# Dense mixtures of a small network: two bank pairs for the sums, high halves on ACT, router from halves, first weights split early

## The reference

```python
# mixture 0 (1 and 3 alike with gelu; 3 has a ninth, shared expert)
logits = jnp.einsum('btc,ce->bte', x, Wg)
probs = jax.nn.softmax(logits, axis=-1)
top_vals, top_idx = jax.lax.top_k(probs, TOP_K)                # TOP_K = 2, 8 experts
gates = (jax.nn.one_hot(top_idx, E, dtype=probs.dtype) * top_vals[..., None]).sum(-2)
h = jax.nn.relu(jnp.einsum('btc,ech->bteh', x, W1) + b1)       # 192 -> 768
y = jnp.einsum('bteh,ehc->btec', h, W2) + b2                   # 768 -> 192
out = jnp.einsum('bte,btec->btc', gates, y)
# mixture 4: (silu(x Wg) * (x Wu)) Wd, 384 hidden channels; mixture 2: capacity 64 per expert
```

## Time and profile before

| | us |
|---|---|
| median of 3 runs | 475.11 |
| lowest and highest run | 474.66, 476.07 |
| profiled execution | 478.6 |
| its span | 476.8 |
| PE matmuls busy in it | 447.4 |
| DVE busy | 337.3 |
| ACT busy | 232.0 |
| POOL busy | 138.4 |

### The profile page before, as it was taken

How to read it: one execution, slowest core, us unless ns; L and a number is a source line. 1 busy time by engine, 2 the same in 40 slices (tenths; PEclk the granted TensorE clock), 3 DMA queues, 4 the chain that set the end, 5 groups by cost and what they waited for, 6 DMA issues and landing times.

```text
span 476.8 us, 9352 instructions
## 1 busy us (share of the span) xinstructions
PE 447.4 (94%) x3260; PEld 385.6 (81%) x3260; DVE 337.3 (71%) x764; ACT 232.0 (49%) x591; POOL 138.4 (29%) x175
## 2 busy tenths in 40 slices
PE   8998999999999899999999897999899999989997
PEld 6776899997676889998677575746699999979997
DVE  3676989995475989996475377421498999887674
ACT  1485455641285665641195058132266565455452
POOL 6011466561011465561001101020055656300000
PEclk9999999999999999999999799999999999999999
DMA  5760155610670155720599403306026566325550
GB/s 156 263 131 2 67 202 154 218 57 1 227 211 1 68 174 174 210 72 0 162 239 246 114 1 92 109 1 231 1 74 211 163 198 197 126 91 182 185 200 20
DMA packets 19364, 62.38 MB, mean 131 GB/s; under 512 B 4041, under 2 KB 6914, under 8 KB 19330
## 3 DMA queue, kind: packets, MB, share of 16 engines
q1 hardware_dynamic: 19330, 61.93, 42.0%
HBM read 59.82 MB, written 2.10 MB: 130 GB/s over the span
## 4 chain that ended last, share of the span: by engine, by line
PE 60%; issue 16%; DVE 7%; ACT 6%; DMA 5%; POOL 3%; SPq 1%; POOLq 0%; DVEq 0%
PE bank L997 23%; PE bank L1005 10%; PE bank L1017 7%; ACT probs L546 5%; PE bank L1019 3%; PE bank L799 2%; PE bank L824 2%; DMA rel<-rel_scratch 2%; PE bank L731 2%; POOL rstd L407 2%; DMA w<-in_M_w_dram 2%; PE bank L692 1%; PE bank L780 1%; PE bank L838 1%; PE bank L974 1%
## 5 line engine op out<-in xcount | busy, mean ns | idle before, releaser
L997 PE MATMUL bank<-xT_hi,w_hi 128*128 128x256 f32 x408 | 109.2, 289 | 1.6 <-issue 1.6
L1282 DVE TENSOR_TENSOR w_lo<-w,w_hi 128x512 fp32r<-128x512 f32 x102 | 96.9, 988 | 2.1
L631 ACT ACTIVATE hid<-bank,b 128x256 f32<-128x256 f32 x150 | 62.8, 471 | 68.7 <-PE bank L997 68.5
L997 PE MATMUL bank<-xT_hi,w_lo 128*128 128x256 f32 x408 | 82.0, 282 | 0.0
L997 PEld LDWEIGHTS bank<-xT_hi,w_hi 128*128 128x128 f32 x408 | 77.9, 191 | 3.9 <-issue 3.8
L460 POOL TENSOR_TENSOR w_hl<-w,consts 128x384 fp32r<-128x384 f32 x50 | 52.5, 1050 | 73.6 <-PE bank L1019 69.9
L997 PEld LDWEIGHTS bank<-xT_hi,w_lo 128*128 128x128 f32 x408 | 63.4, 191 | 0.0
L462 POOL TENSOR_TENSOR w_hl<-w,w_hl 128x384 fp32r<-128x384 f32 x50 | 59.0, 1179 | 3.9
L1005 PE MATMUL bank<-w,hid 128*128 128x192 f32 x308 | 56.4, 327 | 2.5 <-issue 2.5
L583 ACT ACTIVATE w_hi<-w 128x512 fp32r<-128x512 f32 x102 | 58.3, 627 | 0.0
L997 PE MATMUL bank<-xT_lo,w_hi 128*128 128x256 f32 x204 | 57.7, 283 | 0.0
(11 more groups left out here) (169 smaller groups left out, 661.3 us busy)
## 6 DMA issues: line engine op xcount, KB each, us to landing
w<-in_M_w_dram SPq DMA_DIRECT2D x34, 768.0 KB, 5.6
w<-in_M_w_dram SPq DMA_DIRECT2D x33, 576.0 KB, 4.0
w<-in_M_w_dram SPq DMA_DIRECT2D x9, 288.0 KB, 2.9
wqkv<-in_A_wqkv_dram SPq DMA_DIRECT2D x4, 432.0 KB, 7.1
rel_scratch<-relall SPq DMA_DIRECT2D x4, 372.0 KB, 2.3
wproj<-in_A_wproj_dram SPq DMA_DIRECT2D x4, 288.0 KB, 8.3
wqkv<-in_M_w_dram SPq DMA_DIRECT2D x2, 576.0 KB, 23.6
rel<-rel_scratch SPq DMA_DIRECT2D x10, 96.0 KB
```

Of the source, the lines that this page charges most:

```text
L631: ins = act.activation(hid[:, 2 * b + c, :], bank[B_H[b]][:, c * T:(c + 1) * T], FUNC[cfg["act"]], bias=b1[:, kb, bass.ds(at, 1)])
L997: ins = pe.matmul(bank[B_H[b]][:, c2 * T:(c2 + 1) * T], w, xs, start=(q == 0), stop=(q == 4))
L1282: dve.tensor_tensor(w1_cols(w1_lo, b), w1_cols(w1[s], b), w1_cols(w1_hi, b).bitcast(F32), ALU.subtract)\
```

## The change

Five edits, all in the dense mixtures:

1. The sums of even and odd experts go to two bank pairs, (3, 4) and (7, 6). PE waits for the addition of the unit before the last one. In units 0 and 1 DVE makes both units' halves before it adds either sum. The product with the biases b2 moves from bank 6 to 5.
2. `hid_hi` is made by ACT, right after the pair's activation, and no longer by DVE.
3. The router takes the input from `xT_hi` and `xT_lo`, in six matmuls, and the copies to `xT` are gone in dense mixtures.
4. The low half of a mixture's first weights is started ahead of its norm: two parts at the end of attention 0 and 1, all three inside mixture 2 for mixture 3, one at the end of mixture 3 for mixture 4. ACT's high halves stand where they stood.
5. `xn` is written once. The second transpose reads its channels 64 to 191, and the low half of the last 64 channels goes to the lower partitions.

```diff
+EARLY = {0: 2, 1: 2, 3: HB, 4: 1}
...
-        B_H, B_Y, B_R, B_B2 = (0, 1, 2), (3, 4), 5, 6
+        B_H, B_Y, B_R, B_B2 = (0, 1, 2), ((3, 4), (7, 6)), 5, 5
...
@@ ACT: attn, end
+                if n < 2:
+                    for b in range(HB):
+                        split(n, 0, 0, b)
@@ ACT: expert
                             ins.then_inc(h_ready, 1)
+                        if cfg["split2"] and b >= HB - SB:
+                            sb2 = 2 * (b - (HB - SB))
+                            act.wait_ge(h_ready, 3 * (2 * j + g) + b + 1)
+                            act.activation(hid_hi[:, sb2:sb2 + 2, :], hid[:, 2 * b:2 * b + 2, :], ACT.Copy).then_inc(hid_hi_ready, 1)
...
@@ PE: router
+                            terms = ((xT_hi[:, 0, tok].bitcast(F32), 0), (xT_lo[:, tok].bitcast(F32), 0), (xT_hi[:, 1, tok].bitcast(F32), 1))
...
@@ PE: expert
-                    pe.wait_ge(acc_done, 2 * (2 * j + g))
+                    if m or not isinstance(j, int) or j:
+                        pe.wait_ge(acc_done, 2 * (2 * j + g - 1))
...
@@ DVE: ln
-                if m is not None:
-                    split(m, 0, 0, 0)
...
-                    if twice:
-                        ins = dve.tensor_scalar(dst[:, t, C:], src[:, t, P:], moments[:, t, 0:1], rstd[:, t:t + 1],
-                                                ALU.subtract, ALU.mult)
...
@@ DVE: split, early
+            def early(m):
+
+                for b in range(EARLY[m]):
+                    split(m, 0, 0, b)
...
@@ DVE: attn, end
                 turned(5)
+                if n < 2:
+                    early(n)
                 scaled(2)
...
@@ DVE: hidden
-                            dve.wait_ge(h_ready, 3 * (2 * j + BASE[m] + i) + b + 1)
-                            dve.tensor_copy(hid_hi[:, sb2:sb2 + 2, :], hid[:, 2 * b:2 * b + 2, :]).then_inc(hid_hi_ready, 1)
...
+                    if last and m == 3:
+                        early(4)
...
@@ DVE: moe, mixture 2 and the first two units
+                        if ep == EP - 1:
+                            split(3, 0, 0, 0)
+                            split(3, 0, 0, 1)
                         dve.wait_ge(yp_psum, ep + 1)
                         dve.tensor_copy(yplace[:, :], bank[B_YP][:, 0:C]).then_inc(yp_ready, 1)
+                    split(3, 0, 0, 2)
...
-                for i in range(2):
-                    hidden(0, i)
-                    if i == 0:
-                        gate()
-                    add(0, i)
+                hidden(0, 0)
+                gate()
+                hidden(0, 1)
+                add(0, 0)
+                add(0, 1)
```

More of the change, by code:

```diff
@@ L260, in kT_copies, with plain_blocks @@
             return 3 + (2 if by_act else 1) * n
+        def plain_blocks(k):
+            return sum(kind == "attn" or MOE[n]["cap"] for kind, n in BLOCKS[:k + 1])
         def looped(m):
@@ L502, in x_transposed @@
                 kind, n = BLOCKS[k]
-                split_too = kind == "moe" and not MOE[n]["cap"]
-                rows = P if split_too else CH
-                for t in range(TT if split_too else 0):
-                    act.wait_ge(xT_psum, TT * k + t + 1)
-                    act.activation(xT_hi[:, :, t * P:(t + 1) * P], ln_bank(t, P), ACT.Copy).then_inc(xT_hi_ready, 1)
+                if kind == "moe" and not MOE[n]["cap"]:
+                    for t in range(TT):
+                        act.wait_ge(xT_psum, TT * k + t + 1)
+                        act.activation(xT_hi[:, :, t * P:(t + 1) * P], ln_bank(t, P), ACT.Copy).then_inc(xT_hi_ready, 1)
+                    return
                 act.wait_ge(xT_psum, TT * k + 1)
-                if split_too:
-                    act.wait_ge(xT_lo_ready, TT * (split_count(n) - 1) + 1)
                 for c in range(KC if weight is not None else 0):
@@ L514, in x_transposed, with split @@
                 if weight is None:
-                    ins = act.activation(xT[0:rows, :, 0:P], ln_bank(0, rows), ACT.Copy)
+                    ins = act.activation(xT[0:CH, :, 0:P], ln_bank(0, CH), ACT.Copy)
                 ins.then_inc(xT_act, 1)
+            def split(m, j, i, b):
+                s = (i + SHIFT[m]) % 2
+                if b == 0:
+                    act.wait_ge(w1_in[s], 16 * (j + USED[m][s] + 1))
+                act.activation(w1_cols(w1_hi, b), w1_cols(w1[s], b), ACT.Copy).then_inc(w1_hi_ready, 1)
             def attn(n):
@@ L659, in _ @@
             for kind, n in BLOCKS:
[L660 removed]
+                if kind == "moe" and n > 2:
                     for b in range(HB):
@@ L968, in router @@
                 def router():
-                    pe.wait_ge(xT_act, k + 1)
-                    pe.wait_ge(xT_dve, k + 1)
+                    if cfg["cap"]:
+                        pe.wait_ge(xT_act, plain_blocks(k))
+                        pe.wait_ge(xT_dve, plain_blocks(k))
                     for t in range(TT):
-                        for c in range(KC):
-                            rows = CH if cfg["cap"] else (P, CR)[c]
-                            ins = pe.matmul(bank[B_R][:, t * E:(t + 1) * E], xT[0:rows, c, t * P:(t + 1) * P],
-                                            wr[0:rows, m, c, :], start=(c == 0), stop=(c == KC - 1))
+                        tok = slice(t * P, (t + 1) * P)
+                        if cfg["cap"]:
+                            terms = ((xT[0:CH, 0, tok], 0), (xT[0:CH, 1, tok], 1))
+                        else:
+                            terms = ((xT_hi[:, 0, tok].bitcast(F32), 0), (xT_lo[:, tok].bitcast(F32), 0), (xT_hi[:, 1, tok].bitcast(F32), 1))
+                        rows = CH if cfg["cap"] else P
+                        for q, (part, c) in enumerate(terms):
+                            ins = pe.matmul(bank[B_R][:, t * E:(t + 1) * E], part, wr[0:rows, m, c, :],
+                                            start=(q == 0), stop=(q == len(terms) - 1))
                     ins.then_inc(r_psum, 1)
@@ L1011, in halves @@
                         tok = slice(t * P, (t + 1) * P)
-                        out = bank[B_Y[t]]
+                        out = bank[B_Y[i][t]]
                         if last:
@@ L1097, in settle, with ln @@
                 dve.wait_ge(dve_own, own[0])
-            def ln(n, src, eps, dst=xn, twice=False, m=None, src_at=None, first=0):
+            def ln(n, src, eps, dst=xn, src_at=None, first=0):
                 for t in range(first, TT):
@@ L1379, in high @@
                             dve.wait_ge(acc_part, 2 * (2 * j + g - (split_count(m) - 1)) + t + 1)
-                        dve.scalar_tensor_tensor(x[:, t, :], bank[B_Y[t]][:, 0:C], gates[:, t, bass.ds(2 * j + i, 1)],
+                        if not cfg["split2"] or last:
+                            after_last(t)
+                        dve.scalar_tensor_tensor(x[:, t, :], bank[B_Y[i][t]][:, 0:C], gates[:, t, bass.ds(2 * j + i, 1)],
                                                  x[:, t, :], ALU.mult, ALU.add).then_inc(acc_done, 1)
@@ L1444, in _ @@
                 else:
-                    ln(nln, x, (ATTN if kind == "attn" else MOE)[n]["eps"], twice=kind == "moe", m=n if kind == "moe" else None,
-                       src_at=at, first=from_t)
+                    ln(nln, x, (ATTN if kind == "attn" else MOE)[n]["eps"], src_at=at, first=from_t)
                 nln += 1
                 x_transposed(k, LN_WEIGHT.get((kind, n)))
-                for b in range(1, HB if kind == "moe" and n != 2 else 1):
+                for b in range(EARLY[n], HB) if kind == "moe" and n != 2 else ():
                     split(n, 0, 0, b)
```

58 lines of the change are left out of this document (30 added, 28 removed).

## The result

| | before | changed |
|---|---|---|
| median, us | 474.88 (4 runs) | 482.25 (4 runs) |
| lowest and highest, us | 474.64, 476.07 | 481.10, 486.45 |
| profiled execution | 478.6 | 482.11 |
| its span | 476.8 | 480.3 |

The changed kernel takes 1.0157 times as long, 95% interval 1.0124 to 1.0190: slower, as forecast (482.7). PE is busy for the same share of the span; ACT has taken over what DVE gave up.

A forecast was written before the change was run, and what follows sets the result against it. The prediction took PE, never resting in a middle unit, and an equally long loop through ACT and DVE as the bound; 5.3 + 0.3 + 0.15 + 2.15 + 2.1 - 1.5 - 0.9 = +7.6 us gave 482.7, range 474.5 to 487.5.

## What to carry to other kernels

Before work is moved to an idler engine, find the loop that the work stands in. An engine that is busy for half of the time can still be the one that everybody waits for at that place, and what counts there is the length of the step with its handovers, and the start of the next step behind it. Taking away a wait for a result doesn't take away the work behind it: replay the busy engine for one unit more, and look at what it owes then. And a step moved into idle time is free only if its inputs are there; look at who makes them, and when.

## What the runs showed of the hardware

- On ACT the copy of 128x512 in SBUF into the faster type takes 0.63 and lets the next instruction start after 0.54; on DVE the same copy takes 0.41 to 0.47.
- The router's records take 0.10 us each where all loads have 128 rows, and 0.13 where some have 64 (0.79 for 8 and 1.24 for 12, against 1.07 for 8 and 1.52 for 12). At each change between 128 and 64 rows the next load does not overlap the one before it (it starts 0.02 behind its end, else 0.07 to 0.08 before it), and the matmuls are 0.18 to 0.19 apart instead of 0.11; with 96 rows throughout they are 0.11 apart. The Trainium skill (TensorE: Matmul & The Clock Gate, LDWEIGHTS (loading the stationary operand)) says that a load's time goes by its columns and not by its rows. The load records agree, 182 to 192 ns for both heights; the spacing of the matmuls depends on whether the height changes.
- In the part from halves the record behind the fifth comes 0.37 behind it where PE had stopped for the fifth, and 0.28 to 0.34 where it had not. Behind the first one, which follows the second product in full width, it is 0.36 to 0.40 in every kernel.
- A stretch of 6.8 us at a granted clock of 0.50 made attention 3 longer by 3.33 us (29.79 against 26.46), one of 3.4 us by 1.7.
